# The sum of squares of y from a transposed copy, in place of fp32 products with a column of ones

## The reference

```python
q = rmsnorm(q, q_rms_w); k = rmsnorm(k, k_rms_w)
scores = einsum('bthd,bshd->bhts', q, k) * scale + bias[None]      # ALiBi, causal
attn = softmax(scores, axis=-1)
y = einsum('bhts,bshd->bhtd', attn, v)
y = rmsnorm(y, subln_w)              # y * rsqrt(mean(y*y over the 128 of a head) + eps) * w
y = y.transpose(0, 2, 1, 3).reshape(B, T, H * D)
return y @ Wproj
```

## Time and profile before

| | |
|---|---|
| median of 3 runs | 557.12 us (556.85 to 557.29) |
| the profiled execution | 556.8 us |
| its span, first to last instruction | 554.7 us |
| mean granted TensorE clock | 0.991 |
| busy: TensorE, its loads, DVE, ACT, POOL | 531.1, 492.5, 414.6, 376.0, 333.8 us |

### The profile page before, as it was taken

The page is one execution under the profiler, slowest core; times in us unless marked ns, Lnnn a source line. Parts: engine busy times, 40 slices in busy tenths (PEclk is TensorE's granted clock), DMA queues, the critical chain, the costliest instruction groups (busy, mean ns, idle before and its releaser), DMA issues.

```text
span 554.7 us, 12030 instructions
## 1 busy us (share of the span) xinstructions
PE 531.1 (96%) x3548; PEld 492.5 (89%) x3548; DVE 414.6 (75%) x999; ACT 376.0 (68%) x855; POOL 333.8 (60%) x431
## 2 busy tenths in 40 slices
PE   5768999999999999999999999999999999999996
PEld 2758899999989999998999999899999989999885
DVE  5867778686777868777786867778687786878765
ACT  2367778685776868577686857768685776858561
POOL 3386487683748658483776837486584847748121
PEclk9799999999999999999999999999999999999999
DMA  5100101001010100101010010101001000000002
GB/s 159 54 2 1 39 1 38 3 1 40 2 39 0 38 0 0 38 0 38 0 38 0 0 38 0 38 0 32 6 0 38 0 9 0 9 1 1 1 1 77
DMA packets 18582, 10.83 MB, mean 20 GB/s; under 512 B 2176, under 2 KB 18560, under 8 KB 18560
## 3 DMA queue, kind: packets, MB, share of 16 engines
q1 hardware_dynamic: 17568, 10.49, 6.3%
q10 hardware_dynamic: 992, 0.07, 0.1%
HBM read 9.51 MB, written 1.05 MB: 19 GB/s over the span
## 4 chain that ended last, share of the span: by engine, by line
PE 77%; POOL 9%; issue 4%; DVE 3%; ACT 3%; DMA 1%; POOLq 1%; DVEq 0%; SPq 0%
PE pT_ps L551 9%; PE qkv_ps L471 9%; PE qkv_ps L473 8%; PE qkv_ps L472 8%; PE yT_ps L473 6%; PE yT_ps L472 6%; PE yT_ps L471 6%; PE score_big L471 4%; PE score_big L473 4%; PE score_big L472 4%; PE misc L527 3%; POOL qk_n L220 3%; POOL qk_r L385 3%; PE qkv_ps L580 2%; PE yT_ps L580 2%
## 5 line engine op out<-in xcount | busy, mean ns | idle before, releaser
L723 ACT ACTIVATE stage<-qkv_ps 128x384 f32<-128x384 f32 x119 | 58.6, 493 | 91.1 <-PE qkv_ps L473 90.6
L897 DVE TENSOR_TENSOR pT_lo<-pT_ps,pT_hi 128x384 fp32r<-128x384 f32 (+1 forms) x192 | 100.9, 554 | 25.2 <-ACT pT_hi L751 23.3
L751 ACT ACTIVATE pT_hi<-pT_ps 128x384 fp32r<-128x384 f32 (+1 forms) x192 | 86.3, 484 | 46.7 <-PE pT_ps L551 42.9
L425 POOL TENSOR_TENSOR y_r<-y_ms,minus_half 128x4 f32<-128x4 f32 x32 | 32.8, 1026 | 136.1 <-DVE y_ms L913 136.1
L743 ACT ACTIVATE probs<-probs,neg_max 128x1024 f32<-128x1024 f32 (+7 forms) x128 | 98.4, 770 | 8.2 <-DVE neg_max L888 7.6
L551 PE MATMUL pT_ps<-ident,probs 128*128 128x128 f32 x576 | 85.7, 276 | 4.0 <-ACT probs L743 3.3
L471 PE MATMUL qkv_ps<-w_hi,xT_hi 128*128 128x384 f32 x242 | 87.3, 361 | 0.6 <-ACT stage L723 0.6
L473 PE MATMUL qkv_ps<-w_hi,xT_lo 128*128 128x384 f32 x242 | 81.9, 338 | 0.0
L472 PE MATMUL qkv_ps<-w_lo,xT_hi 128*128 128x384 f32 x242 | 81.8, 338 | 0.0
L385 POOL TENSOR_TENSOR qk_r<-qk_ms,minus_half 128x4 f32<-128x4 f32 x64 | 65.0, 1015 | 26.8 <-DVE qk_ms L862 26.0
L551 PEld LDWEIGHTS pT_ps<-ident,probs 128*128 128x128 f32 x576 | 66.8, 143 | 10.9 <-DVE pT_lo L897 4.2
(11 more groups left out here) (182 smaller groups left out, 1308.6 us busy)
## 6 DMA issues: line engine op xcount, KB each, us to landing
w_raw<-in_wq SPq DMA_DIRECT2D x16, 128.0 KB, 2.2
w_raw<-in_wk SPq DMA_DIRECT2D x16, 128.0 KB, 2.3
w_raw<-in_wv SPq DMA_DIRECT2D x16, 128.0 KB, 2.3
wp_raw<-in_wproj SPq DMA_DIRECT2D x16, 128.0 KB, 2.0
acc<-in_x SPq DMA_DIRECT2D x2, 512.0 KB, 5.5
out<-acc SPq DMA_DIRECT2D x8, 128.0 KB, 1.8
w<-in_ffn_w ACTq DMA_DIRECT2D x1, 64.0 KB, 6.2
q_col<-in_q_w ACTq DMA_DIRECT2D x1, 0.5 KB, 3.0
```

Of the source, the lines that this page charges most:

```text
L723: act.activation(stage_of(h, k // 2)[:, k % 2, :], qkv_bank(h, k)[:, 0:3 * D], ACT.Copy).then_inc(qkv_read, 1)
L751: act.activation(pT_hi[g][:, a:b, r * P:(r + 1) * P], pT_ps[(CHUNK0[s] + k) % 2][:, 0:(b - a) * P].rearrange("p (j t) -> p j t", t=P), ACT ...
L897: dve.tensor_tensor(pT_lo[g][:, a:b, r * P:(r + 1) * P], pT_ps[(CHUNK0[s] + k) % 2][:, 0:(b - a) * P].rearrange("p (j t) -> p j t", t=P), ...
```

## The change

ScalarE's first read of yT_ps becomes a plain copy (`y_raw`). TensorE transposes it in four blocks (`turn_y`), so that each row of the result is a query and the head's width lies along the row. ScalarE squares the result from PSUM to `y_sq` (`square_y`, a new instruction), and VectorE reduces it along the row (a new instruction) before it adds the small term. The sums need no `misc_read` count any more: the banks are free when ScalarE has squared, so the waits go to `y_squared`.

Four places in the order change: y_mean of group 0 from step 0 to step 1, y_mean of group 1 from step 4 to step 5 (VectorE), norm_y of group 0 behind split_w, and norm_y of group 1 behind the last norm_qk (GpSimd). The column `ones` goes.

```diff
-            def norm_y(h, g, now):
-                pool.wait_ge(misc_read, misc_done(now, f"ss{g}"))
+            def norm_y(h, g):
+                pool.wait_ge(y_meaned, 2 * h + g + 1)
...
-                if not first:
-                    norm_y(h - 1, 0, h)
                 if tile is not None:
                     round_x(tile)
                 if not (isinstance(h, int) and h + 2 >= H):
                     split_w(h + 2, par)
+                if not first:
+                    norm_y(h - 1, 0)
...
                     split_v(h + 1, 1 - par, NPAIR - 1)
-                if not first:
-                    norm_y(h - 1, 1, h)
                 if not last:
                     norm_qk(h + 1, NPAIR - 1)
+                if not first:
+                    norm_y(h - 1, 1)
...
-            def sum_squares(h, g, now):
+            def turn_y(h, g, now):
                 bank_free(now, f"ss{g}")
-                pe.wait_ge(y_squared, 2 * h + g + 1)
+                pe.wait_ge(y_copied, 2 * h + g + 1)
                 for r in range(4):
-                    last = pe.matmul(job_ps(h + 1, f"ss{g}")[:, r:r + 1], y_sq[:, g, r * P:(r + 1) * P], ones[:, 0:1],
-                                     start=True, stop=True)
-                last.then_inc(ss_ready, 1)
+                    last = pe.transpose(job_ps(h + 1, f"ss{g}")[:, r * P:(r + 1) * P], y_raw[:, g, r * P:(r + 1) * P],
+                                        ident[:, :])
+                last.then_inc(y_turned, 1)
...
-                act.activation(y_sq[:, g, :], yT_ps[:, :], ACT.Square).then_inc(y_squared, 1)
+                act.activation(y_raw[:, g, :], yT_ps[:, :], ACT.Copy).then_inc(y_copied, 1)
                 act.activation(yT_hi[:, g, :], yT_ps[:, :], ACT.Copy).then_inc(y_hi_done, 1)
+
+            def square_y(h, g):
+                act.wait_ge(y_turned, 2 * h + g + 1)
+                past(act, y_summed, 2 * h + g)
+                act.activation(y_sq[:, :], job_ps(h + 1, f"ss{g}"), ACT.Square).then_inc(y_squared, 1)
...
                     if s % 2:
                         exps(h, par, s)
+                    if s == 1 and not first:
+                        square_y(h - 1, 0)
...
                     if s % 2 == 0:
                         exps(h, par, s)
+                    if s == 4 and not first:
+                        square_y(h - 1, 1)
...
                 dve.scalar_tensor_tensor(y_el2[:, g, :], row_sum[:, par, g, :], EPS, row_sum[:, par, g, :],
                                          ALU.mult, ALU.mult).then_inc(el2_ready, 1)
+                dve.wait_ge(y_squared, 2 * h + g + 1)
+                dve.tensor_reduce(y_ms[:, g, :], y_sq[:, :].rearrange("p (r d) -> p r d", d=D),
+                                  AX.X, ALU.add).then_inc(y_summed, 1)
                 dve.wait_ge(el2_ready, 2 * h + g + 1)
-                dve.wait_ge(ss_ready, 2 * h + g + 1)
-                dve.scalar_tensor_tensor(y_ms[:, g, :], job_ps(h + 1, f"ss{g}")[:, 0:4], 1.0 / D, y_el2[:, g, :],
-                                         ALU.mult, ALU.add).then_inc(misc_read, 1)
+                dve.wait_ge(y_summed, 2 * h + g + 1)
+                dve.scalar_tensor_tensor(y_ms[:, g, :], y_ms[:, g, :], 1.0 / D, y_el2[:, g, :],
+                                         ALU.mult, ALU.add).then_inc(y_meaned, 1)
...
+                    if s == 1 and not first:
                         y_mean(h - 1, 1 - par, 0)
...
-                    if s == 4 and not first:
+                    if s == 5 and not first:
                         y_mean(h - 1, 1 - par, 1)
```

More of the change, by code:

```diff
@@ L49, in build_block, with freed @@
     MISC_TAIL = ["ss0", "proj0a", "ss1", "proj0b", "proj1a", "proj1b"]
+    def freed(jobs):
+        return [m for m in jobs if not m.startswith("ss")]
     def misc_done(h, job):
@@ L56, in misc_done @@
             return NPAIR + MISC_FIRST.index(job) + 1
-        base = NPAIR + len(MISC_FIRST) + (h - 1) * len(MISC)
+        base = NPAIR + len(MISC_FIRST) + (h - 1) * len(freed(MISC))
         if isinstance(h, int) and h == H - 1:
-            return base + MISC_LAST.index(job) + 1
+            return base + freed(MISC_LAST).index(job) + 1
         if isinstance(h, int) and h == H:
-            return base - len(MISC) + len(MISC_LAST) + MISC_TAIL.index(job) + 1
-        return base + MISC.index(job) + 1
+            return base - len(freed(MISC)) + len(freed(MISC_LAST)) + freed(MISC_TAIL).index(job) + 1
+        return base + freed(MISC).index(job) + 1
     def past(eng, sem, count):
@@ L81, in build_block @@
         ident_b = sb("ident_b", [P, P], bf16)
-        ones = sb("ones", [P, 1])
         minus_half = sb("minus_half", [P, NT])
@@ L113, in build_block @@
         yT_lo = sb("yT_lo", [P, 2, 4 * P], f32r)
-        y_sq = sb("y_sq", [P, 2, 4 * P])
+        y_raw = sb("y_raw", [P, 2, 4 * P])
+        y_sq = sb("y_sq", [P, 4 * P])
         y_ms = sb("y_ms", [P, 2, 4])
@@ L190, in build_block @@
         y_split = sem("y_split")
-        ss_ready = sem("ss_ready")
+        y_copied = sem("y_copied")
+        y_turned = sem("y_turned")
+        y_summed = sem("y_summed")
+        y_meaned = sem("y_meaned")
         el2_ready = sem("el2_ready")
@@ L251, in squares_of @@
             if isinstance(h, int) and h == 0 and k % 2:
-                return y_sq[:, 0, :].rearrange("p (t n) -> p t n", t=2)
+                return y_raw[:, 0, :].rearrange("p (t n) -> p t n", t=2)
             return squares[:, :, :]
@@ L341, in _ @@
             pool.tensor_copy(ident_b[:, :], ident[:, :]).then_inc(const_ready, 1)
-            pool.memset(ones[:, :], 1.0)
             for h in range(H):
@@ L462, in _ @@
             over_heads(pool, head)
-            norm_y(H - 1, 0, H)
-            norm_y(H - 1, 1, H)
+            norm_y(H - 1, 0)
+            norm_y(H - 1, 1)
         @block.tensor
@@ L492, in bank_free @@
                 same = [m for m in jobs[:jobs.index(job)] if bank_of(h, m) == bank and (m != "ss0" or tail)]
-                if same:
+                if is_last(h) and job == "proj1a":
+                    pe.wait_ge(y_squared, 2 * h - 1)
+                if same and same[-1].startswith("ss"):
+                    pe.wait_ge(y_squared, 2 * h - 1 + int(same[-1][2]))
+                elif same:
                     pe.wait_ge(misc_read, misc_done(h, same[-1]))
@@ L513, in project @@
                 if k == 1 and not (isinstance(h, int) and h <= 1):
-                    pe.wait_ge(misc_read, misc_done(h - 1, "ss0"))
+                    pe.wait_ge(y_squared, 2 * h - 3)
                 for kt in range(KT):
@@ L565, in attend @@
                     if g == 0 and not (isinstance(h, int) and h == 0):
-                        pe.wait_ge(misc_read, misc_done(h, "ss1"))
+                        pe.wait_ge(y_squared, 2 * h)
                     elif g == 0:
@@ L661, in head @@
                             attend(h - 1, 1 - par, 1, 0)
-                            sum_squares(h - 1, 0, h)
+                            turn_y(h - 1, 0, h)
                     if s == 1:
@@ L673, in head @@
                         if s == 4 and not first:
-                            sum_squares(h - 1, 1, h)
+                            turn_y(h - 1, 1, h)
                         elif not first:
@@ L701, in _ @@
             over_heads(pe, head)
-            sum_squares(H - 1, 0, H)
+            turn_y(H - 1, 0, H)
             project_out(H - 1, 1, 0, 0, H)
@@ L706, in _ @@
             project_out(H - 1, 1, 0, 1, H)
-            sum_squares(H - 1, 1, H)
+            turn_y(H - 1, 1, H)
             project_out(H - 1, 1, 1, 0, H)
@@ L840, in _ @@
             probs_hi(H - 1, NT - 1)
+            square_y(H - 1, 0)
             y_out(H - 1, 1)
+            square_y(H - 1, 1)
         @block.vector
@@ L977, in step_of_x @@
                                   ALU.mult).then_inc(x_step_ready, 1)
-            code, sign, mag = y_sq[:, 0, :].bitcast(i32), y_sq[:, 0, :], y_sq[:, 1, :]
+            code, sign, mag = y_raw[:, 0, :].bitcast(i32), y_raw[:, 0, :], y_raw[:, 1, :]
             wide = wb[:, :, :].rearrange("p k i -> p (k i)")
```

## The result

| | before | changed |
|---|---|---|
| median | 556.99 us (4 runs) | 548.26 us (547.63 to 549.33, 4 runs) |
| the profiled execution | 556.8 us | 549.33 us |
| its span | 554.7 us | 547.2 us |

The ratio is 0.9847 (95% interval 0.9828 to 0.9865): faster by 8.7 us, or 1.5%. The prediction was 553.6, so 3.5 us faster, with 546 to 560 as its range. The time lies in the range and on the side forecast, but the gain is two and a half times what was forecast, so the sum was wrong.

The account below looks back on a forecast made before the run. TensorE, busy 96%, and its stalls were taken to bound the kernel. A head: -0.35 - 0.06 + 0.15 = -0.26 us; 14 heads -3.6, last head -0.35, tail +0.5, sum -3.5, hence 553.6 us, range 546 to 560.

Parts of the forecast that it names:

- Group 0: TensorE's turn_y after the first attend half, nothing limiting beside it: transposes in place of fp32 products save 0.35 us.
- Group 1: TensorE's turn_y between project 6 and project 7: saves 0.06 us, the other 0.29 becomes a wait for the copy.
- The added squares: ScalarE's new Square of 128x512, 0.60 us: nothing lost, in group 1 0.50 us of room takes 0.48.
- The first stall: TensorE's 0.51 us wait for qk_n from GpSimd, at 285.22: goes when y_r moves behind qk_n.
- rival 1: The reduction hides in VectorE's waits: a head gains 0.92 us, giving 544.2 us; chance 0.12.
- the term that failed: VectorE's y_mean of group 1 ahead of pT_lo: pT_lo 0.85 us later, the second stall ending 0.15 us later.
- the second stall: TensorE's 0.35 us wait for pT_lo from VectorE, ending at 290.19: to end 0.15 us later, counted from project 7.
- The ends: Last head and tail, outside the 14 loop heads: -0.35 us in the last head, +0.5 in the tail.
- The tail: After the last head, a longer chain of square, reduction, y_ms and y_r puts the adds at 550.7, +0.5 us.
- rival 2: The inserted y_mean takes 1.45 us, by the lock or a late square: +0.34 a head, 561.9 us; chance 0.18.
- Rival 3: No change: group 0's 0.35 us is lost because an earlier projection waits for its copy: 558.5 us; chance 0.2.
- The signs: Trace marks named beforehand: turn_y at 0.44 us, no qk_n waits, pT_lo wait kept or grown, head 0.26 us shorter.

Follow-up runs that it names:

- e6: The changed kernel with the four transposes of turn_y done twice for group 0: 554.75 us.
- e5: The changed kernel with the four transposes of turn_y done twice for group 1: 548.33 us.
- e2: The kernel before, with only GpSimd's order edited: y_r of group 1 behind qk_n of the last pair, sums of squares still fp32 products: 552.10 us.
- e3: The changed kernel with y_mean of group 1 in step 4 and y_r of group 1 ahead of qk_r again: 551.73 us.
- e1: The changed kernel with y_mean of group 1 back in step 4 on the vector engine: 546.44 us.
- e4: The changed kernel with one more 128x512 reduction, result unused, right behind y_mean of group 1 in step 5: 556.12 us.
- e10: The changed kernel with one more 128x512 reduction on the vector engine in step 4, y_mean staying in step 5: 548.58 us.

## Why the prediction was wrong

**TensorE, the exchanged groups: right.** Group 0 was to save 0.35 and saves 0.38, with the transposes behind it; e6 shows that what is added there counts almost in full. Group 1 was to save 0.06, and 0.29 to turn into a wait for the copy of project 6. It saves 0.07, the wait is in the trace, and e5 shows the cover from the other side: four more transposes all but disappear in it.

**ScalarE: right.** The added squares cost nothing that shows in the heads of the loop. The copy of project 7 wasn't late: it starts 1.35 us behind the project's first pass, before (278.82 to 280.17) and after (275.55 to 276.90).

**GpSimd: right in kind, too large in size.** The first stall went through its order alone (e2, e3). It was priced at 0.51 (in rival 1, and in "the 0.51 us won at the first stall doesn't survive") and was worth 0.32 to 0.35 in e2, since I took the bracket of the weight loads for lost time of the matmuls.

**VectorE: the term that failed.** The sum had +0.15 us a head for the end of the second stall, by "From there the vector engine runs without a gap to 287.91". Counted as there, from the start of project 7 (278.82 and 275.55) to the end of the stall (290.19 and 286.70), it is 11.37 before and 11.15 after: -0.22. The error is 0.37 us a head, 5.2 us in 14 heads, against a miss of 5.3; the other errors are smaller and go both ways. By matmul starts the stall's end is only 0.15 earlier (11.38 to 11.23), and 0.08 more come behind it, up to the next group 0.

In the terms of the prediction the +0.15 was a stall of 0.51 won and 0.66 lost again to the reduction. Measured are 0.32 to 0.35 won (e2 against before) and 0.11 to 0.13 lost (e1 against the changed kernel). So the step that failed is the cost of the reduction's place, 0.1 in place of 0.66 us a head. The stall won was overpriced too, and this error hid a part of the first: with the stall at its true worth the same working would have forecast a still slower kernel.

The insertion itself was right (0.81 for 0.85). The run behind it wasn't as dense as it read. Of VectorE before:

```profile
285.65 0.48 DVE L869 SCALAR_TENSOR_TENSOR qT_lo<-qkv_ps,q_col,qT_hi 128x256 fp32r<-128x256 f32 x1
...
286.38 0.68 DVE L888 CUSTOM_DVE_ANT_0 probs<-score_small,bias 128x512 f32<-128x512 f32 x1
...
287.10 0.48 DVE L869 SCALAR_TENSOR_TENSOR qT_lo<-misc,q_col,qT_hi 128x256 fp32r<-128x256 f32 x1
```

Between starts the rows left 0.64 us for the pT_lo of 285.01, which takes 0.47 when nothing holds the next one (282.55 to 283.02, after), and 0.72 for a mask that takes 0.61 (283.74 to 284.35, after). In both places ScalarE's row before the change gives the reason:

```profile
285.23 0.39 ACT L737 ACTIVATE kT_hi<-qkv_ps 128x256 fp32r<-128x256 f32 x1
...
286.66 0.40 ACT L737 ACTIVATE kT_hi<-misc 128x256 fp32r<-128x256 f32 x1
```

The first ends at 285.62, and VectorE's qT_lo of that pair began at 285.65. The second ends at 287.06, and qT_lo began at 287.10. These were waits of 0.17 and 0.11 us for ScalarE, too short for a bracket. Pushed back by 0.8 us, VectorE no longer met them, and with y_mean back in step 4 it meets them again (e1). A last part, near 0.1, is that the adds begin 0.09 before kT_lo ends, where I had put them behind its end. A smaller slip: the follower of the last exponential was worked out as 288.77 and called pT_hi's start, which is 288.82.

**The ends: too good.** They were to give +0.15 and give +0.79. Up to the last yT_hi (547.42 before, 539.02 after) the last head's group 0 is followed by 25.72 us before (from 521.70) and 25.61 after (from 513.41), so 0.11 is saved and not 0.35: y_mean of group 0, which I had let fall "mostly in idle time", comes late enough there that the adds wait for y_r, yT_lo stands behind them, and TensorE waits for yT_lo:

```profile
519.63 0.88 DVE L947 SCALAR_TENSOR_TENSOR acc<-misc,y_r,acc 128x256 f32<-128x256 f32 x2 [0.69 <-POOL y_r L431]
...
521.16 0.19 PEld L477 LDWEIGHTS yT_ps<-wp_hi,yT_hi 128*128 128x128 f32 x1 [0.54 <-DVE yT_lo L926]
```

The tail was to lose 0.5 and loses 0.92. From yT_hi's end to the adds that wait for y_r it is 2.18 us before (548.01 to 550.19) and 3.10 after (539.61 to 542.71). The square waits for the last transposes, and the reduction for the square:

```profile
539.93 0.60 ACT L774 ACTIVATE y_sq<-score_big 128x512 f32<-128x512 f32 x1 [0.32 <-PE score_big L591]
```

```profile
540.56 0.69 DVE L934 TENSOR_REDUCE y_ms<-y_sq 128x4 f32<-128x512 f32 x1 [0.16 <-ACT y_sq L774]
541.36 0.16 DVE L938 SCALAR_TENSOR_TENSOR y_ms<-y_ms,y_el 128x4 f32<-128x4 f32 x1
...
542.71 0.88 DVE L947 SCALAR_TENSOR_TENSOR acc<-qkv_ps,y_r,acc 128x256 f32<-128x256 f32 x2 [0.36 <-POOL y_r L431]
```

Of the 0.42 that were missing, 0.32 are the wait for the transposes, which the prediction had left out. No experiment was made on this part.

**The rivals.** Rival 1, that the reduction hides, is nearer to what happened than the forecast, but its 12.9 us were too many: it too rested on 0.51, and it passed over the round trip that e1 shows. Its sum leaves out the ends (+0.15), and so does rival 2's, though it names them; neither changes a chance. Rival 2's corner is real, and e4 found it, one reduction further on. The long y_el beside GpSimd's qk_n is real too, and didn't meet the new place (0.16 at 281.56). In e1, where y_el stands in step 4 again, it takes its old 0.76 us beside GpSimd's qk_n and harms nothing:

```profile
274.15 1.04 POOL L227 TENSOR_TENSOR qk_n<-stage,qk_r 128x512 f32<-128x512 f32 x1
```

```profile
274.45 0.76 DVE L931 SCALAR_TENSOR_TENSOR y_el<-row_sum 128x4 f32<-128x4 f32 x1
```

Rival 3 falls with e6.

**The signs.** Five came: the rows of turn_y at 0.44 us, the wait for the copy of project 6, no more waits for qk_n, y_mean's rows behind the mask with pT_lo at once behind (0.99 us from y_el to pT_lo, where 0.85 to 0.95 were named), and no bracketed wait of VectorE behind them. Three failed: the waits for pT_lo shrank, the second stall ends 9.80 us behind the start of project 7's copy (276.90 to 286.70) and not 10.2, and the head is 0.70 us shorter and not 0.26. The new waits for kT_lo of the last two pairs did come, but too short for a bracket:

```profile
283.88 0.19 PEld L477 LDWEIGHTS qkv_ps<-wp_hi,yT_hi 128*128 128x128 f32 x1
...
285.28 0.19 PEld L477 LDWEIGHTS score_big<-kT_hi,qT_hi 128*128 128x128 f32 x1
```

The kT_lo that they need end at 283.82 and at 285.16 (284.74 + 0.42). From the output product to the transposes of step 6, and from these to the next head's first scores, TensorE takes 0.76 and 0.46 us before, in e1 and in e2, and 0.81 and 0.60 in the changed kernel, e4 and e10 (means over 11 heads). With 0.02 ahead of the product (2.14 in e1 and e2, 2.16 in the changed kernel, from the last qk transposes) that is 0.21 us. Of it 0.06 come back where the wait for pT_lo is shorter (1.55 to 1.49, from the scores to the transposes of step 7) and 0.04 in what follows, which leaves the 0.11 that the reduction's place costs. The lesson of VectorE's rows holds for TensorE's as well.

## What to carry to other kernels

A run of rows without brackets isn't a run without waits. Before an insertion is priced at its duration, the distances between starts are to be compared with the same operation elsewhere, and each row's start with the end of what it reads on the other engine: waits that short vanish once the engine is later than its supplier. And the bracket before a weight load overstated what TensorE lost: 0.51 us of it were worth 0.32 to 0.35. The distances of matmul starts, over the stall and over the stretch behind it, came nearer (0.23 and 0.07). Where a change exchanges an operation and also moves others, the moves alone are worth a run: here about half the gain (4.8 us of 8.7) was one GpSimd line that the old algorithm could have had.

## What the hardware showed beyond that

Four fp32 transposes and four fp32 products of one column differ by a factor of two in TensorE's time (0.43 and 0.81 us a group), though their results have 512 and 4 columns: the trace counts eight passes for the products and four for the transposes, each about 0.1 us, at a mean granted clock of 0.99.
